# TensorE's order at the end of an attention block with a mixture layer: both remaining output projections ahead of the first transposes and logits

## What is computed

```python
h = _layernorm(x) * (1 + ca) + sa
x = x + ga * attention(h)            # ends in: out @ Wo.T, summed over 32 heads
h = _layernorm(x) * (1 + cb) + sb
logits = einsum('th,eh->te', h, router_weight) + router_bias     # 64 experts
topk_w, topk_idx = top_k(softmax(logits), 8)
out = h * topk_w.sum() + einsum('te,eh->th', w_dense, expert_bias)
x = x + gb * out
```

## Time and profile before

| | |
|---|---|
| median of 3 runs | 1459.76 us (1459.34 to 1461.4) |
| the profiled execution, its own time | 1460.17 us |
| its span, first to last instruction | 1458.9 us |
| PE busy in the span | 1431.4 us (98%) |
| DVE, ACT, POOL busy | 1154.3, 1007.9, 1023.6 us |
| mean granted TensorE clock | 0.999 |

### The profile page before, as it was taken

One profiled execution on the slowest core, in us unless ns is written; L12 is line 12 of the kernel. 1 busy time (PEld: TensorE's weight loads), 2 busy tenths in 40 slices (PEclk: granted clock), 3 DMA queues, 4 the chain that ended last, 5 costly groups with the idle time before them and its releaser, 6 DMA issues.

```text
span 1458.9 us, 24651 instructions
## 1 busy us (share of the span) xinstructions
PE 1431.4 (98%) x7150; PEld 1208.2 (83%) x7150; DVE 1154.3 (79%) x3544; ACT 1007.9 (69%) x2389; POOL 1023.6 (70%) x805
## 2 busy tenths in 40 slices
PE   7989999999999999999999999999999999999998
PEld 7877888888888888888888888888888888888876
DVE  5697777787777777777777777777779989888876
ACT  5667666766676676777676677676667677776673
POOL 3768766776676677677676677676588888886662
PEclk9999999999999999999999999999999999999999
DMA  9478766775677767676587668658878989899881
GB/s 308 162 210 248 219 203 182 238 230 167 198 224 206 198 213 229 195 212 201 177 234 217 216 180 225 193 170 263 236 232 264 268 285 285 262 265 268 267 234 48
DMA packets 215157, 322.03 MB, mean 221 GB/s; under 512 B 42512, under 2 KB 132464, under 8 KB 215024
## 3 DMA queue, kind: packets, MB, share of 16 engines
q1 hardware_dynamic: 214736, 320.39, 73.2%
q10 hardware_dynamic: 288, 0.07, 0.0%
HBM read 179.43 MB, written 140.95 MB: 220 GB/s over the span
## 4 chain that ended last, share of the span: by engine, by line
PE 88%; DVE 4%; POOL 2%; DMA 2%; issue 2%; ACT 2%; SPq 1%; DVEq 0%; ACTq 0%
PE bank_s L633 22%; PE bank_o L793 22%; PE bank_pv L743 14%; PE bank_s L699 13%; PE bank_s L665 5%; PE bank_s L650 5%; PE bank_s L695 1%; POOL PT_lo L1835 1%; PE bank_s L606 1%; PE bank_s L849 1%; DVE y L1539 1%; DVE blocks L1487 0%; PE bank_s L696 0%; DMA wc_scratch<-wc_out 0%; PE bank_o L606 0%
## 5 line engine op out<-in xcount | busy, mean ns | idle before, releaser
L1835 POOL TENSOR_TENSOR PT_lo<-PT_raw,PT_hi 128x640 fp32r<-128x640 f32 x246 | 382.4, 1577 | 30.1 <-ACT PT_hi L1125 30.1
L1111 ACT ACTIVATE probs<-probs,row_inv 128x512 f32<-128x512 f32 (+3 forms) x512 | 257.8, 553 | 193.9 <-DVE row_inv L1470 193.7
L1823 POOL TENSOR_TENSOR rot_c<-rot_c,rot_s 128x512 f32<-128x512 f32 x128 | 167.3, 1307 | 256.8 <-DVE rot_s L1427 256.8
L1104 ACT ACTIVATE probs<-probs,row_min 128x384 f32<-128x384 f32 (+3 forms) x512 | 281.6, 552 | 48.6 <-DVE row_min L1463 48.5
L1487 DVE STREAM_TRANSPOSE blocks<-probs 128x384 f32<-128x384 f32 x508 | 213.8, 446 | 19.7 <-ACT probs L1111 14.1
L699 PE MATMUL bank_s<-kT_both,qT_hi 128*128 128x512 f32 (+2 forms) x768 | 215.2, 341 | 2.7 <-DVE row_min L1463 1.0
L1463 DVE CUSTOM_DVE_ANT_0 probs<-bank_s,mask 128x512 f32<-128x512 f32 (+2 forms) x384 | 205.4, 552 | 0.8 <-issue 0.3
L1828 POOL TENSOR_TENSOR qT_lo<-rot_c,qT_hi 128x512 fp32r<-128x512 f32 x128 | 166.8, 1304 | 50.8 <-ACT qT_hi L1086 49.9
L793 PE MATMUL bank_o<-wo_lo,OT_hi 128*128 128x512 f32 x496 | 195.7, 394 | 2.2 <-DMA wo_lo<-split_wo 1.7
L633 PE MATMUL bank_s<-hT_lo,wq_hi 128*128 128x512 f32 x484 | 194.8, 403 | 2.2 <-DVE row_min L1463 1.4
L793 PE MATMUL bank_o<-wo_hi,OT_hi 128*128 128x512 f32 x496 | 194.1, 391 | 0.0
(11 more groups left out here) (315 smaller groups left out, 3255.8 us busy)
## 6 DMA issues: line engine op xcount, KB each, us to landing
blocks<-blocks SPq DMA_DIRECT2D x127, 640.0 KB, 3.4
PT_raw<-blocks SPq DMA_DIRECT2D x500, 160.0 KB, 3.9
stage<-in_wq SPq DMA_DIRECT2D x32, 256.0 KB, 5.1
vblocks<-kv_raw SPq DMA_DIRECT2D x32, 256.0 KB, 5.4
kv_raw<-vblocks SPq DMA_DIRECT2D x128, 64.0 KB, 2.2
stage<-in_wo SPq DMA_DIRECT2D x32, 256.0 KB, 5.1
split_wq<-wq_hi SPq DMA_DIRECT2D x32, 256.0 KB, 5.2
split_wq<-wq_lo SPq DMA_DIRECT2D x32, 256.0 KB, 5.5
```

The costliest lines, as they stand in the source:

```text
L1104: ins = act.activation(row(t, qt), row(t, qt), ACT.Exp, bias=row_min[m][:, qt:qt + 1], scale=-1.0, accum_out=row_sum[m][:, qt:qt + 1])
L1111: ins = act.activation(row(t, qt), row(t, qt), ACT.Copy, scale=row_inv[t % 2][:, qt:qt + 1])
L1823: pool.tensor_tensor(rot_c[:], rot_c[:], rot_s[:], ALU.add).then_inc(pool_a, 1)
L1835: pool.tensor_tensor(lo[:, at], raw_of(t)[:, at], hi[:, at].bitcast(F32), ALU.subtract).then_inc(pool_t, 1)
```

## The change

PE's program at the end gets another order. Both tiles of `out_pair` go first, in one call, then the last two heads' projections of tile 2, the transposes of a, the last two heads' projections of tile 3, the transposes of b, and then the logits of a and b one after the other. No instruction is added or taken away, and no other engine's program is changed.

```diff
             a, b, c, d = range(EARLY_TILES, TILES)
-            out_pair(PAIRS - 1, UPPER, [2])
-            ffn_transpose(a, "pv")
+            out_pair(PAIRS - 1, UPPER)
             out_last(ALL - 1, 2)
             out_last(ALL - 2, 2)
-            ffn_logits(a, "s1")
-            out_pair(PAIRS - 1, UPPER, [3])
-            ffn_transpose(b, "s3")
+            ffn_transpose(a, "pv")
             out_last(ALL - 1, 3)
             out_last(ALL - 2, 3)
+            ffn_transpose(b, "s3")
+            ffn_logits(a, "s1")
             ffn_logits(b, "s2")
             ffn_transpose(c, "pv")
             tile_waits((bias, a))
```

## The result

The changed kernel takes 1463.62 us (median of 13 runs, 1461.56 to 1468.51), the kernel before 1460.95 us on 13 runs that include the three shown ahead (1459.34 to 1462.83). The ratio is 1.0021, its 95% interval 1.0013 to 1.0029: slower by 1.9 to 4.2 us, clear of no change. The interval is 0.08% to either side, so the 0.2% that the prediction called measurable was too cautious a bound. The forecast was 1461.1 us within 1459.7 to 1463.2, "within 0.2%" at 0.81. The time lies outside the range. 1.2 us of the miss is the anchor: three runs of before had a lower median than thirteen (1459.76 against 1460.95), and from the median of thirteen the same range would have ended at 1464.4. The rest is in the kernel: +2.7 us of medians and +2.8 us in the profiled spans (1461.7 against 1458.9), where +1.37 was forecast.

The account below looks back on a forecast made before the run. PE was busy 98%, but the end was taken as bound by a relay of PE, DVE and ACT queues. Logits of a ending at 1442.21 put the bias +1.37 us later: 1459.76 + 1.37 = 1461.1 us, range 1459.7 to 1463.2.

Parts of the forecast that it names:

- Steps 1 to 6: End stretch on PE, ACT and DVE, from projections of c to logits of a: bias of a 1.37 us later.
- the early bank of d: Projections of d ready 3.1 us earlier, expected to buy nothing; as a rival, end at 1456.7 us, chance 0.02.
- Step 7: Everything behind the bias of a, stores included, shifts as one piece by 1.37 us.
- a sign of being wrong: A tail not shifted as one piece would mean a wait in it hung on something not seen.
- the clock: TensorE's granted clock may fall at about 1443 to 1446, PE being thinly loaded; cost 0 to 2.6 us, middle +1.2.
- clock high or its fall nearly free: Case of the timetable shift alone, end at 1460.9 to 1461.5 us; chance 0.55.
- a fall with a price: Clock falls and delays the end: under 1.55 us (to 1462.6), chance 0.20; more than that, chance 0.14.
- the rival: Clock fall on PE between 1443 and 1448 costs 0.3 to 2.6 us more: 1462.3, at most 1463.7; chances 0.20 and 0.14.
- the gain of 0.3 us: DVE's earlier start on c reaches the end, 1459.4 us; chance 0.09 together with "no change".
- no change: Nothing moved reaches the end, 1459.8 us; chance 0.09 together with the gain of 0.3 us.

Follow-up runs that it names:

- kernel 2: Changed kernel with the logits of a moved ahead of the transposes of b on PE; ratio 1.0010 to the kernel before.
- kernel 3: Changed kernel with ACT's normalisation of b moved ahead of its modulation of a; ratio 1.0019 to the kernel before.
- kernel 7: Kernel before with only both tiles of out_pair put in front in one call; ratio 1.0000 to the kernel before.
- kernel 1: Changed kernel with nine unread 512-column matmuls between the logits of a and of b; ratio 1.0007 to the kernel before.
- kernel 5: Changed kernel with three unread 512-column matmuls in the 0.90 us hole ahead of the transposes of b; ratio 1.0017 to the kernel before.
- kernel 6: Changed kernel with four unread 512-column matmuls between the logits of a and of b; ratio 1.0005 to the kernel before.
- kernel 8: Changed kernel with DVE's begin of d moved ahead of the bias and selection of a; ratio 1.0030 to the kernel before.
- kernel 9: Changed kernel with logits of a ahead of transposes of b, and seven unread matmuls ahead of logits of b; ratio 1.0000 to the kernel before.

## Why the prediction was wrong, step by step

- **Steps 1 to 6** held. c's bank gained 0.3 us (DVE took it up 4.38 us behind `out_pair`'s start instead of 4.70), the transposes of a came 1.56 us later (forecast 1.57), ACT's modulation of a held back the normalisation of b, the new hole of 0.9 us is 0.90, the early bank of d (1439.30 + 0.40 = 1439.70) bought nothing, and the bias of a is 8.61 - 7.25 = 1.36 us later (forecast 1.37). Kernels 2 and 3 show the two links by taking each away, kernel 7 that tile 3's move was covered.
- **Step 7**, the rest of the timetable shifts as one piece: right only where the clock holds, as in the profiles of kernels 1, 5 and 6 (tails longer by 1.37, 1.35 and 1.36 us). In the changed kernel the tail was not shifted as one piece, which the text had named as a sign of being wrong.
- **The step that failed is the clock.** The text found the thin stretch and its length (1.5 us of work in 4.6), called the fall "as likely as not" and then made the time of the case without it the forecast, with 0.55 for "clock high or its fall nearly free" and 0.34 for a fall with a price. In the profile of the changed kernel the clock was at 0.50 from 1443.0 to 1449.9, and all 13 runs have a mean clock of 0.997 or less, which 11 of 88 runs of before have. With the text's own +1.2 for the fall the shift would have been 1.37 + 1.2 = 2.57 us, and the medians lie 2.67 apart. The measured 1463.62 us is also within the price that the rival was given (at most 1463.7); the range had cut that end off.
- **Its price was mis-sized at the lower end.** +1.2 was the value, 0 to 2.6 the bounds; measured 25.37 - 23.83 = 1.54 us, just at the 1.55 from which it was to decide, with 6.9 us at the low level, and 0.58 and 0.79 us in kernels 2 and 3 with 3.4 us of it. The open question, whether groups of 64 and 128 columns are slowed by the clock at all, is answered: from logits of b to the transposed weights of a PE took 1446.90 - 1444.28 = 2.62 us instead of 1.38, +1.24 where +1.2 was worked out with the factor of 512 columns. ACT passed on 1.17 of it (normalisation of d at 1449.23, 2.53 us later by `out_pair`'s clock, 1.36 of which is the order's). The remaining 0.4 us come from PE's own queue: rows of a (1.57 us instead of 0.82) and the mixing behind them, also slow, pushed the logits of c back, and these, at nearly full pace again (0.93 us), kept the transposes of d until 1450.61. A fall that is "nearly free" came in no profile; what chance it had been given belonged to the falls with a price.
- **The rule of the Trainium skill** that the prediction cited, "TensorE: Matmul & The Clock Gate", section "LDWEIGHTS (loading the stationary operand)", has no term for the clock, and by it short groups would have kept their pace and the sum would have been +1.4. The trace does not agree, and it decides: at the 1.2 GHz level the eight logits took 1.77 us, 0.22 us each, against 0.11 at full clock, and the tail is 2.9 us longer.
- **The other rivals**: the gain of 0.3 us ended in DVE's wait of 1.68 us, as the text against it said; the bank of d is excluded further by kernel 8; "no change" is excluded by the interval.

What the fall hangs on exactly stays open. The share of low runs goes with the idle time that is left to PE: 13 of 13 with holes of 2.19 and 0.90 us, 10 and 7 of eleven with 2.19 and the smaller one nearly closed (kernels 3 and 5), 7 with 1.74 (kernel 2), 4 with 1.59 (kernel 7), 1 with 1.20 (kernel 6), none with the hole filled (1 and 9). But the profiles of kernels 3 and 5 have the same hole of 2.19 us with waits of no more than 0.21 us in the work ahead of it, and in one the clock fell and in the other it did not; which execution falls is not told by anything that the runs show.

## What to carry to other kernels

Before work is moved into a hole of one engine, ask which member of each other engine's queue stands behind the work that is pushed back: here a modulation that came 1.5 us later held a normalisation that did not depend on it, and that one the logits. Move only what has no slack (tile c's projections), and leave the rest where it filled the shadow of another engine. And a hole in TensorE's work near the end is not only idle time: price the clock for everything behind it, short matmuls included, and read the clock of many runs, since one profile can show either kind.

## What was not expected of the hardware

- Matmuls of 64 and 128 columns take almost twice as long at the 1.2 GHz level, like those of 512: eight logits 1.77 us instead of 0.91 to 0.94, eight `ffn_rows` 1448.68 - 1447.11 = 1.57 us instead of 0.82.
- The clock stayed at 0.50 for almost 7 us (1443.0 to 1449.9) though PE was busy from 1444.28 on; in kernels 2 and 3 it came back after about 3.4 us, and in the earlier trace rows the 3.7 us with a mean of 0.57 hold some 3.2 us of it, (1 - 0.57) / 0.5 x 3.7. The short matmuls behind the fall do not explain the longer stretch: kernel 3's earlier one lasted 7 us as well, with projections of 512 columns behind it.
- Nine matmuls that nobody needs shortened the tail by 1.54 us; four did the same (1.55).
